# Moving the second half of the value layer's first step into the compressed tiles of its own image

## The reference, cut to what matters

```python
def _mlp(x, w1, b1, w2, b2):
    return jax.nn.gelu(x @ w1 + b1, approximate=False) @ w2 + b2
k_cmp = _mlp(kpos, cmpk_w1, cmpk_b1, cmpk_w2, cmpk_b2)
v_cmp = _mlp(fv, cmpv_w1, cmpv_b1, cmpv_w2, cmpv_b2)      # fv: 225 blocks x 2048
g = _sigmoid(_gelu(xs @ gate_w1 + gate_b1) @ gate_w2 + gate_b2)
```

## Time and profile before

| | |
|---|---|
| median of 3 runs | 748.17 us (747.45 to 748.37) |
| the profiled execution | 749.96 us, its span 748.2 us |
| TensorE, VectorE, ScalarE, GpSimd busy | 662.0, 439.9, 443.2, 233.8 us |
| mean granted clock of TensorE | 0.952 of full speed |
| opening / images' stages / experts (from the chain) | 0 to 58 / 58 to 545 / 545 to 748 us |

### The profile page before, as it was taken

The page is one execution under the profiler, slowest core; times in us unless marked ns, Lnnn a source line. Parts: engine busy times, 40 slices in busy tenths (PEclk is TensorE's granted clock), DMA queues, the critical chain, the costliest instruction groups (busy, mean ns, idle before and its releaser), DMA issues.

```text
span 748.2 us, 16869 instructions
## 1 busy us (share of the span) xinstructions
PE 662.0 (88%) x5318; PEld 496.9 (66%) x5318; DVE 439.9 (59%) x1429; ACT 443.2 (59%) x1287; POOL 233.8 (31%) x341
## 2 busy tenths in 40 slices
PE   2997899999899999989999999877899998989992
PEld 1694467666557766555776656554468897989981
DVE  4206847553986754488676548777646653455443
ACT  1307844664883366487336648633767896878961
POOL 3200014200202473110247310042605477644551
PEclk9999999999999999989999998985899999999995
DMA  7301000000000010000001090001301334363215
GB/s 293 126 0 30 1 1 6 2 0 29 29 2 2 4 35 25 29 1 1 3 4 37 24 264 18 1 5 48 77 8 38 132 86 103 84 200 93 73 47 179
DMA packets 36353, 40.03 MB, mean 54 GB/s; under 512 B 12176, under 2 KB 27936, under 8 KB 35980
## 3 DMA queue, kind: packets, MB, share of 16 engines
q1 hardware_dynamic: 30412, 27.47, 12.8%
q0 software_dynamic: 4704, 9.40, 3.8%
q10 hardware_dynamic: 1152, 2.10, 0.8%
HBM read 25.64 MB, written 15.17 MB: 55 GB/s over the span
## 4 chain that ended last, share of the span: by engine, by line
PE 62%; DVE 16%; ACT 9%; issue 5%; DMA 3%; SPq 2%; POOL 2%; DVEq 1%; ACTq 0%; POOLq 0%
PE ps L1713 8%; PE ps L1788 8%; PE ps L1830 6%; PE ps L1773 6%; PE ps L2173 6%; PE ps L1718 5%; PE ps L2191 5%; PE ps L1860 3%; ACT r_P L927 3%; DVE nmx L1241 2%; PE ps L1890 2%; PE ps L1933 2%; PE ps L1875 2%; PE ps L1902 1%; DVE r_P L1251 1%
## 5 line engine op out<-in xcount | busy, mean ns | idle before, releaser
L927 ACT ACTIVATE r_P<-ps,nmx 128x225 f32<-128x225 f32 (+1 forms) x192 | 86.0, 468 | 62.6 <-DVE nmx L1241 62.6
L1241 DVE TENSOR_REDUCE nmx<-ps 128x4 f32<-128x900 f32 (+1 forms) x64 | 73.7, 1156 | 24.7 <-PE ps L1830 24.1
L778 POOL DMA_INDIRECT xs_d<-pay,pos x64 | 62.4, 974 | 35.9 <-DVE nmx L1241 20.8
L800 POOL DMA_INDIRECT z_d<-xhatT,xrow_room x54 | 52.7, 977 | 61.9 <-DVE xhatT L1632 55.2
L702 POOL TENSOR_TENSOR rstd<-vpe,minus_half 128x8 f32<-128x8 f32 x8 | 13.6, 1701 | 187.0 <-DVE vpe L1178 187.0
L1713 PE MATMUL ps<-ident,r_P 128*128 128x128 f32 (+1 forms) x384 | 54.6, 284 | 13.0 <-DVE R L1263 7.7
L1713 PEld LDWEIGHTS ps<-ident,r_P 128*128 128x128 f32 (+1 forms) x384 | 45.7, 152 | 26.7 <-issue 9.8
L1620 DVE TENSOR_TENSOR hv<-ps,x_sb 128x128 f32<-128x128 f32 x78 | 22.7, 291 | 67.8 <-PE ps L2191 51.4
L752 POOL TENSOR_TENSOR r_gh<-r_gh,nmw 113x392 f32<-113x392 f32 (+1 forms) x20 | 15.6, 781 | 140.5 <-DVE nmw L1280 140.3
L1788 PEld LDWEIGHTS ps<-r_vc,w_sb 128*128 128x128 f32 x256 | 46.1, 188 | 19.4 <-issue 15.9
L1788 PE MATMUL ps<-r_vc,w_sb 128*128 128x225 f32 x256 | 58.8, 375 | 0.0
(11 more groups left out here) (242 smaller groups left out, 1461.6 us busy)
## 6 DMA issues: line engine op xcount, KB each, us to landing
xrow_room<-xs_d SPq DMA_DIRECT2D x54, 65.0 KB, 2.0
x_sb<-x SPq DMA_DIRECT2D x4, 512.0 KB, 3.5
w_sb<-w1k SPq DMA_DIRECT2D x1, 2048.0 KB, 7.6
w_sb<-w1v SPq DMA_DIRECT2D x1, 2048.0 KB, 12.1
w_sb<-fw SPq DMA_DIRECT2D x1, 2048.0 KB, 9.7
w_sb<-fw SPq DMA_DIRECT2D x4, 512.0 KB, 10.0
r_vw<-z_d SPq DMA_DIRECT2D x8, 256.0 KB, 4.0
out<-x_tok ACTq DMA_DIRECT2D x8, 256.0 KB, 2.2
```

The costliest lines, as they stand in the source:

```text
L778: gp.indirect_dma_start(xs_d, bass.IndirectOffsetOnAxis(pos[:, NT * k + t:NT * k + t + 1], 0), pay[:, k, t, :], None).then_inc(scattered, 16)
L800: gp.indirect_dma_start(z_d, bass.IndirectOffsetOnAxis(xrow(n)[:, C + 1:C + 2].bitcast(U32), 0), yrow(n), None).then_inc(y_out[n % XRING], 16)
L927: last = sc.activation(Pb[t % NRING][:, h, 0:m], bank(name)[:, (h % 2) * m:(h % 2) * m + m], ACT.Exp, bias=nmx[:, t % NRING, h:h + 1], acc ...
L1241: ve.tensor_reduce(nmx[:, t % NRING, :].rearrange("p (a h) -> p a h", a=2), v.rearrange("p a (h m) -> p a h m", h=2), AX.X, ALU.max, negat ...
```

## The change

The second half of the value layer gets a bank of its own (`mw`, bank 6) and is made in steps 0 to 3 of the image's own compressed tiles, four steps to a tile, two and two between the other extras. The selected tiles and the opening keep the first half: two steps a tile. While `mw` holds bank 6 (steps 0 to 3), all other extras go to bank 7 alone; from step 4 on to 7 and 6 in turn. The gates' logits get a tile of their own (`gg`, step 0, for image 0 too). Gelu of the second half runs on ScalarE in step 4, the second product in step 5 (`gv`); in exchange the queries of the selected branch go from step 5 to 4, `gc` from 4 to 6, two parts of the window queries one step later. SyncE waits for `mw` of image 3 instead of `mv` before it loads the experts' weights.

```diff
+MW_SLOTS = 4
...
-        extra = around((6, 7))
+        put(6, f"mw@{b}")
         for t in range(NT + F_LAG):
+            if t == 0:
+                extra = around((7,))
+            if t == MW_SLOTS:
+                extra = around((7, 6))
...
-    late_head = {0: ("gv", "kw0"), 1: ("kw1",), 4: ("kw2",)}
-    own = {1: ("vw0",), 4: ("gc0", "gc1"), 5: ("qs0", "qs1", "qw0"), 6: ("qw1",), 7: ("vw1", "qw2"),
-           8: ("gb",), 10: ("vw2", "vw3", "gw0", "gw1")}
-    names = [f"Oc0@{b}"] if t == O_LAG + 1 else []
+    late_head = {0: ("kw0",), 1: ("kw1",), 4: ("kw2",)}
+    own = {1: ("vw0",), 4: ("qs0", "qs1"), 5: ("gv", "qw0"), 6: ("gc0", "gc1"), 7: ("vw1", "qw1"),
+           8: ("gb", "qw2"), 10: ("vw2", "vw3", "gw0", "gw1")}
+    names = [f"Oc0@{b}"] if t == O_LAG + 1 else [f"gg@{b}"] if t == 0 else []
...
-                    sp.wait_ge(*copied(f"mv@{b + 1}"))
+                    sp.wait_ge(*copied(f"mw@{b + 1}"))
...
+            def hidden_values(h, a):
+                name = f"{('mv', 'mw')[a]}@{h}"
+                act.wait_ge(*filled(name))
+                sc.activation(hv[:, a, :], bank(name)[:, 0:NB], ACT.Gelu, bias=col(f"b1v{a}")).then_inc(read_sem(name), 1)
...
-                hidden_from_bank("mk@0", hk, [b1k[:, a:a + 1] for a in range(2)])
-                hidden_from_bank("mv@0", hv, [col(f"b1v{a}") for a in range(2)])
+                hidden_keys_from_bank(0)
+                hidden_values(0, 0)
                 key_blocks(0)
-                gate_exp(0)
...
                         if prev >= 0:
                             window_keys(b, 2)
-                        gates_by_channels(b, "gc", g_cmp)
-                    if t == 5:
+                        hidden_values(b, 1)
                         for i in range(2):
                             queries(f"qs{i}@{b}", qTs, i, 1)
+                    if t == 5:
                         window_queries(b, 0)
...
                         hidden_keys_in_place(h)
-                        hidden_from_bank(f"mv@{h}", hv, [col(f"b1v{a}") for a in range(2)])
+                        hidden_values(h, 0)
...
-                compressed_values_and_gates(0)
-                gates(0)
...
                     if t == 0 and prev >= 0:
                         row_variances(EPS_T)
-                        compressed_values_and_gates(b)
...
+                    if t == 0:
+                        gate_logits(b)
+                    if t == 3:
                         gates(b)
...
+                    if t == 5:
+                        compressed_values(b)
...
+            def value_part(h, t, j):
+                at_ = NPOS + NPOS // MW_SLOTS * t + NPOS // MW_SLOTS // 2 * j
+                value_layer(h, range(at_, at_ + NPOS // MW_SLOTS // 2))
...
-                value_layer(0, range(2 * NPOS))
+                value_layer(0, range(NPOS))
...
-                compressed_values_and_gates(0)
...
-                    if t == 0 and prev >= 0:
-                        compressed_values_and_gates(b)
-                        pe.wait_ge(xwin_ready, b + 1)
-                        window_projection(b, "kw", 1, 0)
+                    if t == 0:
+                        gate_logits(b)
+                        value_part(b, t, 0)
+                        if prev >= 0:
+                            pe.wait_ge(xwin_ready, b + 1)
+                            window_projection(b, "kw", 1, 0)
+                        value_part(b, t, 1)
                     if t == 1:
                         if prev >= 0:
                             window_projection(b, "kw", 1, 1)
+                        value_part(b, t, 0)
+                        value_part(b, t, 1)
                         window_values(b, 0)
+                    if t == 2:
+                        for i in range(2):
+                            if prev >= 0:
+                                router_input(prev, i)
+                            value_part(b, t, i)
                     if t == 3:
-                        if h < B:
-                            image_by_tokens(h)
+                        for i in range(2):
+                            if h < B:
+                                image_by_tokens(h, i)
+                            value_part(b, t, i)
                         if prev >= 0:
                             router_logits(prev)
                     if t == 4:
                         if prev >= 0:
                             window_projection(b, "kw", 1, 2)
-                        gates_by_channels(b, "gc", 0)
+                        slc_queries(b)
                     if t == 5:
-                        slc_queries(b)
+                        compressed_values(b)
                         window_projection(b, "qw", 0, 0)
...
                     if t < NT and h < B:
-                        value_layer(h, range(4 * t, 4 * t + 4))
+                        value_layer(h, range(2 * t, 2 * t + 2))
```

More of the change, by code:

```diff
@@ L1028, in compressed_tiles @@
                         gates_by_rows(b)
+                        window_queries(b, 2)
                     if t == 9 and h < B:
@@ L1196, in window_keys, with gate_logits, compressed_values @@
                 last.then_inc(read_sem(name), 1)
-            def compressed_values_and_gates(h):
+            def gate_logits(h):
+                name = f"gg@{h}"
+                dve.wait_ge(*filled(name))
+                for j in range(NT // NQ):
+                    at_ = 3 * NQ * j
+                    last = ve.tensor_tensor(ge[:, j:NT:NT // NQ, :], bank(name)[:, at_:at_ + 3 * NQ].rearrange("p (q g) -> p q g", g=3),
+                                            rows[:, ROW_GB:ROW_GB + 3].unsqueeze(1).to_broadcast([128, NQ, 3]), ALU.add)
+                last.then_inc(read_sem(name), 1)
+            def compressed_values(h):
                 name = f"gv@{h}"
                 dve.wait_ge(*filled(name))
-                for j in range(NT // NQ):
-                    at_ = 2 * C + 3 * NQ * j
-                    ve.tensor_tensor(ge[:, j:NT:NT // NQ, :], bank(name)[:, at_:at_ + 3 * NQ].rearrange("p (q g) -> p q g", g=3),
-                                     rows[:, ROW_GB:ROW_GB + 3].unsqueeze(1).to_broadcast([128, NQ, 3]), ALU.add)
                 ve.tensor_tensor(v_sb[:, 0, :], bank(name)[:, 0:C], rows[:, ROW_B2V:ROW_B2V + C], ALU.add)
@@ L1486, in compressed_tiles @@
                         payload(prev)
-                    if t == 3 and prev >= 0:
+                    if t == 0:
+                        gate_logits(b)
+                    if t == 3:
                         gates(b)
@@ L1721, in pixels, with image_by_tokens @@
                 return xhatT[:, 16 * i:16 * i + 16, :]
-            def image_by_tokens(h):
+            def image_by_tokens(h, i):
                 pe.wait_ge(x_in, h * 16 + 16)
-                for i in range(2):
-                    transposes(f"xt{i}@{h}", [x_sb[:, 512 * i + 128 * j:512 * i + 128 * j + 128] for j in range(4)], 128, 128)
+                transposes(f"xt{i}@{h}", [x_sb[:, 512 * i + 128 * j:512 * i + 128 * j + 128] for j in range(4)], 128, 128)
             def normalised_image(h):
@@ L1785, in value_layer @@
                             pe.wait_ge(*copied(f"vc{i}@{h}"))
-                        claim(f"mv@{h}")
+                    if s == 0:
+                        claim(name)
                     r, c = divmod(s, KS)
-                    last = mm(bank(f"mv@{h}")[:, NB * a:NB * a + NB],
+                    last = mm(bank(name)[:, 0:NB],
                               w1v_sb[:, s, C * a:C * a + C], vcT[:, r:r + 2 * NBH - 1:2, c:c + 2 * NBH - 1:2],
                               start=(s == 0), stop=(s == NPOS - 1))
-                    if step == 2 * NPOS - 1:
-                        last.then_inc(full_sem(f"mv@{h}"), 1)
+                    if s == NPOS - 1:
+                        last.then_inc(full_sem(name), 1)
+            def value_part(h, t, j):
+                at_ = NPOS + NPOS // MW_SLOTS * t + NPOS // MW_SLOTS // 2 * j
+                value_layer(h, range(at_, at_ + NPOS // MW_SLOTS // 2))
             def compressed_keys(h):
@@ L1812, in compressed_values_and_gates, with compressed_values @@
                 for j in range(NT // NQ):
-                    at_ = 2 * C + 3 * NQ * j
-                    mm(bank(name)[:, at_:at_ + 3 * NQ], gh[:, 128 * j:128 * j + 128], gw2_sb[:, :],
-                       start=True, stop=True)
+                    at_ = 3 * NQ * j
+                    last = mm(bank(name)[:, at_:at_ + 3 * NQ], gh[:, 128 * j:128 * j + 128], gw2_sb[:, :],
+                              start=True, stop=True)
+                last.then_inc(full_sem(name), 1)
+            def compressed_values(h):
+                name = f"gv@{h}"
                 pe.wait_ge(*copied(f"mv@{h}"))
+                pe.wait_ge(*copied(f"mw@{h}"))
+                claim(name)
                 pe.nop(nofuse=True)
@@ L1941, in third_branch_by_tokens, with router_input @@
                 last.then_inc(full_sem(f"pj{j}@{b}"), 1)
```

(10 more changed lines are left out.)

30 lines of the change are left out of this document (16 added, 14 removed).

## The result

The changed kernel takes 759.12 us in the median of four executions (757.99 to 761.22), where the kernel before took 748.27 on the same chip: 1.0145 times as long, 95% interval 1.0114 to 1.0175. Measured once more in a later job, with 20 executions of the kernel before beside it, it was 1.0112 (1.0067 to 1.0158), some 8 us. The forecast was 750.8 with a range up to 757, so the direction was the forecast one and the size was not.

A forecast was written before the change was run, and what follows sets the result against it. TensorE, busy 662.0 of 748.2 us, was taken as the bound; opening -7.5, selected tiles -17.4, compressed tiles +23.9 and clock +3.6 summed to +2.6, giving 750.8 us; likeliest case 748 to 755, full range 737 to 757.

The forecast's parts named there:

- Opening: Before the first maximum: half the value layer (6.7 us) and the gates' work (0.8) come off, -7.5 us.
- selected tiles: Images 0 to 2: two value steps fewer take 0.83 us off each of seven tiles, -17.4 us in all.
- rival E: Selected tiles: the round with two value steps takes 3.2 us instead of 2.94, 756.3 us in all; chance 0.05.
- The chain of the loss: Compressed tiles: bank 7 claims, then waits through Gelu and queries to tile 3's first chunk; +23.9 us over four images.
- the price of the low clock: TensorE's queries behind the wait for Gelu run at a lower clock: 0.9 us an image, +3.6, ends 0 and +4.9.
- Steps 0 to 3: Compressed tiles of image 1: the half layer and single bank 7 cost +3.0 us, ends +2.0 and +6.2.
- two claims "that wait in earnest": Bank 7, steps 0 to 3: first window keys await the logits' read (0.24 us), second router transposes their predecessor's (1.72).
- Steps 4 to 6: Image 1: bank waits, Gelu and table loads bring the loss at tile 6's maximum to +6.7 us, +7.1 with window queries.
- the clock's high end: Upper end of the clock term at the queries: 1.2 us an image, +4.9 for four images.
- B: Rival at the pause before the queries: window keys keep the clock up, sum -1.0, 747.2 us; chance 0.20.
- C: Rival in steps 0 to 6: VectorE's order sets the pace, bank chain hidden, sum -11.6, 736.6 us; chance 0.26.
- D: Rival on ScalarE: eight table switches each cost about 1.3 us beyond the load, 10 more, 761 us; chance 0.06.

The follow-up runs named there:

- the two runs on the bank: Changed kernel with 14 of 16 second-half steps left out, bank kept: 757.93 us; with the second half and its bank left out: 731.48 us.

## Why the prediction was wrong

*The two gains were right:* Opening -7.5 against -8.2, selected tiles -17.4 against -17.1. The round in the selected tiles (rival E) did not bind: 2.94, not 3.2.

*The chain of the loss was right as well.* As forecast: single bank, logits' read, last window keys, table load, Gelu, queries, transposes, chunk, second load, exponentials: each stands in the trace in that order, and the queries run at half clock behind it.

*The step that failed is the price of the low clock.* The prediction took 0.9 us an image, 3.6 in all: half of the queries were to run behind the clock's return, and the transposes that queue behind them were left out of the term. Measured against 1.98 for the queries and 1.04 for the transposes at full clock, the two took 1.5, 2.7, 1.6 and 2.7 us longer in the four images, 8.5 in all, and 6.7 in the second profile. In image 1 all of this lies on the way to the first chunk of tile 3, for which VectorE waits. The run that kept TensorE busy shows the clock to be a cause and not only a sign: it gave back 6 to 9 us.

*The other terms of the loss, by contrast, nearly hold in sum.* Less the clock, 34.3 is 25.8 us and the second profile's 32.1 is 25.4, where 23.9 was forecast.
- **Steps 0 to 3**: +3.0 at the fifth maximum of image 1, measured 3.8. The prediction reckoned from TensorE's work (17.2 us into 13) and added two claims "that wait in earnest"; both are in the trace, 1.40 and 1.07. That the size came out near is in part luck: in image 1 the loss is 4.2 without the work (at a lower clock), and none without work and bank. In image 0 the reckoning by work holds.
- **Steps 4 to 6**: +3.7 from the fifth to the seventh maximum of image 1; measured 6.2, of which 2.7 are the clock, so 3.5. The first chunk of tile 3 was to come 6.3 late, without the clock, and came 9.6 late, counted from the read of the gates' logits (207.10 behind 185.34 before, 209.16 behind 177.84 after): 2.7 of the difference are the clock, and nearly all of the rest is that of steps 0 to 3.

*The range was too narrow* for the same reason: the clock's high end, 4.9 for four images, was all of the queries' slowing and still nothing for the transposes, and the range was drawn around the value taken.

*The rivals.* The stretch at 0.50 speaks against B (clock stays up), the time and the two runs on the bank against C (bank chain hidden). D gave the nearest time, 761, by a mechanism that isn't there: in the rows of ScalarE above, a load of 1.28 starts at 202.69, and the Gelu at 203.98, with no pause. The drain of 1380 ns that the Trainium skill, "ScalarE: Activation LUTs", section "What ACT_TABLE_LOAD costs", states beside the load is not in these rows; the measurement decides, and the load alone stands.

What stays open: how the times behind the seventh maximum divide among the late read-outs in step 7 and 8; what the half layer's work costs where the extras keep two banks, and so whether a third bank for the extras would make the whole change free. Neither was tried.

## What to carry to other kernels

When an accumulation is to hold a PSUM bank over several steps, price what the bank did in that time, and not only the matmuls: here the rotation of two banks became a single file, and each claim waited for the read-out before it. Two runs show whether the bank alone is enough for a loss: leave out the work and keep the bank, then leave out both. Read the granted clock in each, since a kernel with work left out can have a lower one. Where TensorE will pause, price the low clock over all the work that queues behind the pause, not over the first matmuls alone. And a read-out that needs another function table belongs where no engine has a tile's work queued behind it; a claim that waits moves on to the next claim of the same late bank until the reader itself is early.

## What the runs showed of the hardware

In image 1 TensorE paused for 1.58 and for 2.86 us, with 0.68 us of work between. The granted clock was 0.50 from 203.0 us, inside the second pause, to 209.8, and the four projections took 3.78 instead of 1.98. In the second profile the same pauses had a stretch at 0.50 from 205.3 to 208.7, and 3.43. Without table loads the pauses were 1.59 and 1.43: behind them the projections took 3.67 in image 1 and 1.99 in image 2, so the lengths of the pauses alone did not settle it. Repeated matmuls of 2.54 us in the second pause kept the clock at 1.00 and gained 0.9% to 1.2% of the kernel's time. A kernel with less work for TensorE had the lower clock in more places (0.73 and 0.63 in two stretches, 41.0 us at 0.50 between 60 and 475 us against 23.9) and was no faster. A table load took 1.28 us, with 0.02 us between the read-out before it (201.67 + 1.00) and its start at 202.69, and 0.01 between its end and Gelu.
